# A graph layer's edge sort: joining the pieces of destination and weight on GpSimd instead of VectorE

## What is computed

```
hi, hj = h[src], h[dst]                       # 50000 rows each
x   = concat(hi, hj, edge_weight)
msg = layer_norm(silu(x @ mW1 + mb1))
msg = silu(msg @ mW2 + mb2)
agg = segment_sum(msg, src)                   # 3125 rows
y   = silu(concat(h, agg) @ uW1 + ub1) @ uW2 + ub2
```

## Time and profile before

| what | value |
|---|---|
| three executions | 1671.7, 1673.52, 1680.5 us |
| median | 1673.52 us |
| span of the profiled execution, first to last instruction | 1439.5 us |
| the profiled execution's own time | not listed apart from the three |
| median less span | 234.0 us |
| mean granted TensorE clock | 0.950 |

### The profile page before, as it was taken

How to read it: one execution, slowest core, us unless ns; L and a number is a source line. 1 busy time by engine, 2 the same in 40 slices (tenths; PEclk the granted TensorE clock), 3 DMA queues, 4 the chain that set the end, 5 groups by cost and what they waited for, 6 DMA issues and landing times.

```text
span 1439.5 us, 32698 instructions
## 1 busy us (share of the span) xinstructions
PE 1279.5 (89%) x8927; PEld 1149.6 (80%) x8928; DVE 1182.8 (82%) x3550; ACT 932.1 (65%) x1856; POOL 878.1 (61%) x885
## 2 busy tenths in 40 slices
PE   2678899996999999999999999999998847999990
PEld 1366778786999999999999999999886635988890
DVE  6999778726999999999999999999954688666662
ACT  0877444414778887888878888888753544666660
POOL 2188774035887778787777787878710014767761
PEclk7599999997999999999999999999999978999995
DMA  3911100022333333333333333336860162444447
GB/s 118 197 34 43 31 13 23 1 68 64 111 104 98 104 106 101 101 99 112 99 101 102 107 103 101 100 108 93 86 193 0 43 253 72 75 73 73 73 60 280
DMA packets 71387, 133.94 MB, mean 93 GB/s; under 512 B 23126, under 2 KB 43868, under 8 KB 70695
## 3 DMA queue, kind: packets, MB, share of 16 engines
q0 software_dynamic: 36560, 77.33, 24.1%
q1 hardware_dynamic: 33986, 52.62, 12.0%
q10 hardware_dynamic: 780, 3.24, 0.6%
HBM read 107.71 MB, written 25.29 MB: 92 GB/s over the span
## 4 chain that ended last, share of the span: by engine, by line
PE 71%; DVE 17%; DMA 4%; issue 3%; ACT 2%; POOL 1%; DVEq 0%; ACTq 0%; POOLq 0%; SPq 0%
PE ps L1071 12%; PE ps L832 9%; PE ps L1045 7%; PE ps L1049 7%; PE ps L1044 7%; PE ps L1061 7%; DVE place_val_t L1579 3%; DVE lane_hot_e_t L1574 2%; PE ps L1170 2%; PE ps L1201 2%; PE ps L1199 2%; PE ps L1200 2%; PE ps L1172 2%; PE ps L1171 2%; PE ps L1102 2%
## 5 line engine op out<-in xcount | busy, mean ns | idle before, releaser
L752 POOL DMA_INDIRECT msg_t<-dst_table,stage_idx x448 | 444.2, 991 | 128.7 <-issue 126.5
L1044 PE MATMUL ps<-w_hi_t,msg1T_hi_t 128*128 128x256 f32 x896 | 252.4, 303 | 0.0
L1338 ACT ACTIVATE msg1n_t<-msg_t,nw_b,nw_y 128x256 f32<-128x256 f32 x448 | 242.4, 590 | 0.0
L1350 ACT ACTIVATE msg_t<-msg_t 128x512 f32<-128x512 f32 x224 | 141.6, 632 | 149.4 <-DVE msg_t L1743 148.8
L1045 PE MATMUL ps<-w_lo_t,msg1T_hi_t 128*128 128x256 f32 x896 | 234.2, 283 | 0.0
L1071 PE MATMUL ps<-msg_t,hot_t 128*125 128x256 f32 x896 | 230.4, 379 | 0.2 <-issue 0.2
L1049 PE MATMUL ps<-w_hi_t,msg1T_lo_t 128*128 128x256 f32 x896 | 179.8, 282 | 0.0
L1045 PEld LDWEIGHTS ps<-w_lo_t,msg1T_hi_t 128*128 128x128 f32 x896 | 171.9, 192 | 0.0
L1044 PEld LDWEIGHTS ps<-w_hi_t,msg1T_hi_t 128*128 128x128 f32 x896 | 170.3, 190 | 0.0
L1738 DVE BATCH_NORM_STATS2 est<-msg_t 128x6 f32<-128x256 f32 x448 | 166.2, 413 | 1.2 <-ACT msg_t L1350 1.2
L1071 PEld LDWEIGHTS ps<-msg_t,hot_t 128*125 128x125 f32 x896 | 152.0, 187 | 14.2 <-issue 0.4
(11 more groups left out here) (374 smaller groups left out, 3081.1 us busy)
## 6 DMA issues: line engine op xcount, KB each, us to landing
near_rows<-row_list SPq DMA_DIRECT2D x44, 320.0 KB
w_sb_t<-in_L_ffn_W_dram SPq DMA_DIRECT2D x16, 512.0 KB, 8.5
msg_t<-dst_table,stage_idx POOLq DMA_INDIRECT x448, 2.8
res_t<-in_x_dram SPq DMA_DIRECT2D x1, 3125.0 KB
total<-zero_chunks_t SPq DMA_DIRECT2D x1, 3125.0 KB, 26.8
dst_table<-dst_stage SPq DMA_DIRECT2D x25, 125.0 KB
xm_table<-xm_t POOLq DMA_DIRECT2D x5, 625.0 KB, 7.5
sum_a_t<-total SPq DMA_DIRECT2D x5, 625.0 KB, 10.6
```

The source lines that it names most:

```text
L752: pool.indirect_dma_start(out=msg1[:, k, j, :], out_offset=None, in_=dst_table, in_offset=bass.IndirectOffsetOnAxis(stage_idx[:, G * k + j ...
L1044: pe.matmul(o[j], part(msg1T_hi, j, c), w2_hi[:, c, :], start=(c == 0), stop=False)
L1338: m = A(msg1n[:, (kl + 1) % 2, j, :], msg1[:, kk, j, :], ACT.Identity, bias=nw_b[:, kk, j:j + 1], scale=nw_y[:, kk, j:j + 1])
L1350: A(v, v, ACT.Silu).then_inc(msg1_sb, 1)
```

## The change

The three additions of `land(g)` move from VectorE to GpSimd, with a semaphore `landed` of their own. GpSimd's program becomes: for each group g, `land(g)`, then the three scatters numbered 3g-3 to 3g-1 (`BESIDE` is 3; none ahead of group 1); behind the loop the remaining scatters, 45 to 111. `part_w` gets two buffers at another place. ScalarE's copies of group g wait for `landed` of g-2. SP's row loads and VectorE's source table wait for all sixteen landings. The halves of the chunk numbers are summed in PSUM: two matmuls of one column for each run, 14 a group instead of seven of two columns, so VectorE has one addition left (`chunk_places`) and `run_to` goes. Two semaphores of the expert routing (`gap_ok`, `exp_ok`) become one, `softmax_ok`, with two values.

```diff
-        part_w = sort_use("part_w_t", [128, PLACES], F32)
+        part_w = at("part_w_t", [128, 2, PLACES], F32, "work", 15872)
...
@@ sync
             sp.wait_ge(chunk_ok, GROUPS)
-            sp.wait_ge(chunk_ps, GROUPS)
+            sp.wait_ge(landed, GROUPS)
...
@@ gpsimd
             pool.wait_ge(zeros_out, 16)
+
+            def land(g):
+                in_chunks = lambda t: t.rearrange("p (j c) -> p j c", c=CHUNK)
+                pool.wait_ge(sort_ok, g + 1)
+                st.did(pool.tensor_tensor(part_w[:, g % 2], pieces[:, g % 2, 3], pieces[:, g % 2, 4], ALU.add))
+                st.did(pool.tensor_tensor(sort_sb[:, g, :, :, 0], in_chunks(pieces[:, g % 2, 0]), in_chunks(pieces[:, g % 2, 1]),
+                                          ALU.add))
+                st.join()
+                pool.tensor_tensor(sort_sb[:, g, :, :, 2], in_chunks(part_w[:, g % 2]), in_chunks(pieces[:, g % 2, 5]), ALU.add)\
+                    .then_inc(landed, 1)
+
+            def scatter(g, j):
+                pool.wait_ge(landed, g + 1)
+                pool.wait_ge(chunk_ok, g + 1)
+                pool.indirect_dma_start(
+                    out=sorted_edges, out_offset=bass.IndirectOffsetOnAxis(chunk_to[:, g, j:j + 1], 0),
+                    in_=sort_sb[:, g, j].rearrange("p c f -> p (c f)"), in_offset=None).then_inc(scattered, 16)
+
+            BESIDE = 3
             for g in range(GROUPS):
-                pool.wait_ge(sort_ok, g + 1)
-                pool.wait_ge(chunk_ok, g + 1)
-                for j in range(RUNS):
-                    pool.indirect_dma_start(
...
+                land(g)
+                for q in range(BESIDE * g - BESIDE, BESIDE * g):
+                    if q >= 0:
+                        scatter(q // RUNS, q % RUNS)
+            for q in range(BESIDE * GROUPS - BESIDE, GROUPS * RUNS):
+                scatter(q // RUNS, q % RUNS)
@@ tensor
                 for j in range(RUNS):
-                    m = pe.matmul(bank(4 + g % 2, 2, first=2 * j), reached[0:NB + 1, g % 2, j * 128:j * 128 + 128],
-                                  group_h[0:NB + 1, g, :], start=True, stop=True)
+                    for h in range(2):
+                        m = pe.matmul(bank(4 + g % 2, 1, first=j), reached[0:NB + 1, g % 2, j * 128:j * 128 + 128],
+                                      group_h[0:NB + 1, g, h:h + 1], start=(h == 0), stop=(h == 1))
@@ scalar
                 act.wait_ge(sort_ps, g + 1)
-                after(act, chunk_ok, g - 1)
+                after(act, landed, g - 1)
@@ vector
-            def land(g):
...
+            def chunk_places(g):
                 dve.wait_ge(chunk_ps, g + 1)
-                ends = bank(4 + g % 2, 2 * RUNS).rearrange("p (j h) -> p j h", h=2)
-                st.did(dve.tensor_tensor(run_to[:], ends[:, :, 0], run_row[:], ALU.add))
-                st.join()
-                dve.tensor_tensor(chunk_to[:, g], ends[:, :, 1], run_to[:], ALU.add).then_inc(chunk_ok, 1)
+                dve.tensor_tensor(chunk_to[:, g], bank(4 + g % 2, RUNS), run_row[:], ALU.add).then_inc(chunk_ok, 1)
...
                 if g:
-                    land(g - 1)
-            land(GROUPS - 1)
+                    chunk_places(g - 1)
+            chunk_places(GROUPS - 1)
             dve.wait_ge(zeros_out, 16)
             dve.wait_ge(total_zero, 16)
+            dve.wait_ge(landed, GROUPS)
```

More of the change, by code:

```diff
@@ L329, in gps_layer @@
         run_row = s("run_row", [128, RUNS])
-        run_to = s("run_to", [128, RUNS])
         token = s("token", [128, TOPK * NB])
@@ L400, in gps_layer @@
             "reached_ok", "sort_in", "sort_ps", "sort_ok", "chunk_ps", "chunk_ok"))
-        scattered, table_ps = sem("scattered"), sem("table_ps")
+        scattered, landed, table_ps = sem("scattered"), sem("landed"), sem("table_ps")
         table_sb, side_out, xnT_lo_ok, w_hi_ok, w_lo_ok = (sem(n) for n in (
@@ L432, in gps_layer @@
             "var2_ok", "sd2_ok", "rstd2_ok", "xm_ok", "x2T_ps", "x2T_sb", "logit_ps"))
-        gap_ok, exp_ok, hotk_ok, route_ps, tile_ok = (sem(n) for n in (
-            "gap_ok", "exp_ok", "hotk_ok", "route_ps", "tile_ok"))
+        softmax_ok, hotk_ok, route_ps, tile_ok = (sem(n) for n in ("softmax_ok", "hotk_ok", "route_ps", "tile_ok"))
+        GAP_OK, EXP_OK = 1, 2
         logit_ok = sem("logit_ok")
@@ L1405, in _ @@
                 copy_xm(t, t // 4 + 1)
-            act.wait_ge(gap_ok, 1)
-            A(wtmp[0:NP], wtmp[0:NP], ACT.Exp).then_inc(exp_ok, 1)
+            act.wait_ge(softmax_ok, GAP_OK)
+            A(wtmp[0:NP], wtmp[0:NP], ACT.Exp).then_inc(softmax_ok, 1)
             act.wait_ge(w2_in, 16 * NE)
@@ L1553, in _ @@
             step(dve.tensor_tensor(edge(place_h), by_col(place_i), by_col(place_j), ALU.add))
-            def land(g):
[L1556 to L1559, removed]
-                st.did(dve.tensor_tensor(sort_sb[:, g, :, :, 2], part_w[:].rearrange("p (j c) -> p j c", c=CHUNK),
-                                         piece(5), ALU.add))
+            def chunk_places(g):
                 dve.wait_ge(chunk_ps, g + 1)
-                ends = bank(4 + g % 2, 2 * RUNS).rearrange("p (j h) -> p j h", h=2)
-                st.did(dve.tensor_tensor(run_to[:], ends[:, :, 0], run_row[:], ALU.add))
-                st.join()
-                dve.tensor_tensor(chunk_to[:, g], ends[:, :, 1], run_to[:], ALU.add).then_inc(chunk_ok, 1)
+                dve.tensor_tensor(chunk_to[:, g], bank(4 + g % 2, RUNS), run_row[:], ALU.add).then_inc(chunk_ok, 1)
             st.join()
@@ L1856, in _ @@
             st.join()
-            dve.tensor_tensor(wtmp[R], top_v[R, :, 1], top_v[R, :, 0], ALU.subtract).then_inc(gap_ok, 1)
+            dve.tensor_tensor(wtmp[R], top_v[R, :, 1], top_v[R, :, 0], ALU.subtract).then_inc(softmax_ok, 1)
             for k in range(TOPK):
@@ L1890, in _ @@
             st.did(dve.tensor_copy(slot_t[R], slot_q[R, 1]))
-            dve.wait_ge(exp_ok, 1)
+            dve.wait_ge(softmax_ok, EXP_OK)
             step(dve.tensor_scalar(wgt[R, 0, :], wtmp[R], 1.0, None, ALU.add))
```

2 lines of the change are left out of this document (removed).

## The result

The changed kernel takes 1680.94 us (median of 15 runs, 1673.45 to 1685.97), the kernel before, run beside it on the same chip, 1672.11 us (15 runs, 1665.47 to 1681.75). The ratio is 1.0051 [1.0031, 1.007]: the change costs about 9 us. The forecast was 1676.0 in a range of 1667 to 1682.

A forecast was written before the change was run, and what follows sets the result against it. The prediction took VectorE to bound the sort; its -6.5 us goes uncollected because GpSimd would end last, so +3.0 - 0.5 = +2.5 us on 1673.52 gave 1676.0 us, range 1667.0 to 1682.0.

The forecast's parts named there:

- Removed 0.61 a group: Sort, VectorE: moving the additions saves 0.61 us a group, 9.2 us over fifteen groups, the most the change can give.
- The port cost of three additions: Sort, VectorE: GpSimd's reads for 45 additions, priced by columns, cost VectorE 2.7 us, leaving it a net -6.5 us.
- The third rival: Sort: shared-port rule to the letter, VectorE loses each whole addition, 13.5 - 9.2 = +4.3 us, 1677.8; chance 0.07.
- matmuls at nothing: Sort, TensorE: seven more one-column matmuls add at most 0.2 us a group, hidden by its wait for place_val.
- So POOL becomes what ends the sort: 166.7: Sort's end: GpSimd's last landing at 166.7 us, against VectorE's src_lo start at 163.68 today: +3.0 us.
- the first rival: Sort: GpSimd keeps up in phase, last landing at 157.2, VectorE's gain of up to 6.5 us collected, 1667.0 to 1670.5; chance 0.22.
- The tail. ... The cover is 21 us; nothing to pay.: After the sort: last scatter at 255.8, table landed at 261.4, ScalarE reads it at 282.57, so the delay costs nothing.
- All later stages shift one for one: Stages after the sort: they keep their length and move by as much as the sort's end moves.
- The signs: Wrong if GpSimd's last landing comes before 158, its additions take over 0.6 us, or stages after the sort change length.
- 234.0 us "around the span": Whole kernel: the profiled span of 1439.5 us plus 234.0 us around it gives the median, 1673.52, untouched by the change.

The follow-up runs named there:

- pe_only: Kernel before, with only TensorE summing the halves of the chunk numbers and the three additions kept on VectorE: 1675.09 us, ratio 1.0026.
- base: The kernel before, unchanged, profiled once more: 1672.74 us, ratio 1.0012; the profiled execution has a span of 1675.0 us.
- land_only: Changed kernel with the chunk numbers as before and two buffers for run_to, so only the additions move to GpSimd: 1679.28 us, ratio 1.0051.
- beside0: Changed kernel with BESIDE = 0, all 112 scatters behind the sixteenth landing: 1730.77 us, ratio 1.0376.
- The pair with the bound: At most two scatters in flight, kernel before from group 8, changed kernel from its 46th scatter: 1604.52 us (0.9581) and 1612.43 us (0.9642).
- hold: Kernel before, with GpSimd waiting for the whole source table ahead of the scatters of group 8: 1657.06 us, ratio 0.9916.

## Why the prediction was right and wrong

**Right: VectorE's terms.** Removed 0.61 a group was 0.62. The port cost of three additions, priced by columns at 0.18 a group, was 0.23 (3.00 - 2.77). The end of place_val came 4.8 us earlier (152.9 against 157.7), where 6.5 was the sum over fifteen groups. The third rival, the rule to the letter, is refuted: the three additions last 0.25 + 0.56 + 0.42 = 1.23 on GpSimd and cost VectorE 0.23, not their whole length. (The Trainium skill, "SBUF — State Buffer", "Who interferes with whom", calls the shared port pair an exclusive lock. These rows agree that both sides wait: two of the three additions take 0.56 and 0.42 beside VectorE's products, all three of the last landing, with VectorE idle, 0.25. But VectorE does not lose the whole of what the profile records as the addition's length. The Trainium skill says "for the whole instruction" there of VectorE's two-port modes; of an instruction with both inputs in SBUF it says only that it contends.)

**Right as far as shown: matmuls at nothing.** pe_only has no longer period, and the landings alone cost what the change costs; pe_only's ratio of 1.0026 leaves room for a few us.

**Wrong: "So POOL becomes what ends the sort: 166.7".** The last landing ended at 157.6. A landing cost 1.26 and not 1.63: 16 x 0.37 = 5.9 us. I had taken the odds of meeting a VectorE instruction as if the two ran independently; they fell in phase, the first rival's condition, with its 157.2. And the count of scatters up to the last landing was 42, not 45, since `land(15)` stands ahead of the scatters 42 to 44: 3 x 1.62 = 4.9 us. Together that more than covers the 9.1 us of difference. So the sort went as rival 1 had it, though its 157.2 was met partly by luck: it too counts 45 scatters, and it takes 1.04 for a landing that cost 1.26; put right, the sum is 67.67 + 42 x 1.62 + 16 x 1.26 = 155.9. By that rival the time would have been faster; it was not, because of the next step.

**Wrong, and deciding: "The tail. ... The cover is 21 us; nothing to pay."** The landing of the table was the only thing that I let the last scatter delay. The runs show another: as long as scatters leave every 1.26 to 1.29 us, TensorE's counts reach ScalarE late, and the stage beside them stands. In base that stage ends 25 us behind the last scatter (231.3 to 256.2), so this end has no cover at all. The seventy scatters behind the last landing (67 in the prediction, by the same slip in the count), 1.29 us each, end at 247.7 (I had 255.8), which is 16.4 us after base's 231.3, and keys and values start 11.9 us later. The gain of the sort, 4 to 5 us, is lost in it: a tile that is ready earlier waits longer. What shows it are the starts of keys and values in seven profiles (11 us apart, as said above), land_only (same cost) and beside0 (last scatter 67 us later, time 60 us later). The pair with the bound shows that the crawl costs at least 4% of the time; it does not show that the change's loss goes with it, since 0.6% of it stays.

**"All later stages shift one for one"** held for keys and values (92 us in both), not for the source table (87 and 110 us).

**The signs.** Of the three that were to show the prediction wrong, two came: the last landing before 158 (157.6), and a stage after the sort that changed length. The third did not: no addition of the steady pattern took over 0.6 us (0.56).

**The ground.** The prediction was built on an execution in which the crawl doesn't show, though its scatters were nearly as dense (1.34 us apart on the mean of the tail), and I added 234.0 us "around the span" without asking what they were. In base only 1.8 us are around it, and the spans differ by 235.5 us, of which 82.0 are there when the edge loop starts (417.9 against 335.9) and 154.7 are added in it. A gap of 14% between span and time meant that the profile wasn't one of the timed executions, and that some stage took longer in those. It could be seen before. What makes an execution crawl or not was not found; that the old trace is the only complete one is a difference on record.

## What to carry to other kernels

Count what a change adds to the queue that ends last, even where its result is wanted late: the row of indirect DMAs disturbed whoever ran beside it. Where an engine idles on a "remote" release in a program of one core, look for a dense row of DMAs with completion counts, and try to space them out or to bound those in flight; here a few lines of waits on two semaphores brought 4% in the executions measured, many times what the change was after. Look first whether the trace is complete: here it was not wherever the crawl was. And a profile whose span is far from the median of the runs is to be taken again before anything is summed on it.

## What was not expected of the hardware

- In the traced executions a count of TensorE went up as much as 58 us after its matmul while scatters were issued every 1.26 us, each raising a count by 16 on completion (`then_inc(scattered, 16)`); ScalarE's counts for VectorE and VectorE's for TensorE took about 0.1 us at the same time (168.89 to 169.03, 169.45 to 169.51). That the sixteen increments of each scatter are what TensorE's stand behind is compatible with all runs (density, hold, bound), but no run shows where a count waits, or that it would wait without the recording. The Trainium skill, "DMA: Bandwidth & Descriptors", section "Why a DMA increments its semaphore by 16 and not by 1", says that all 16 DMA engines post a +1 for a DMA issued by GpSimd; the complete old trace agrees, with 1792 changes for 112 scatters.
- While the stage crawls, the clock falls to its lower level (the windows of base, 160 to 240 us: TensorE busy 14.03 of 80 us, granted clock 0.55 on the mean; from 168 to 240 us it is busy 9.89 of 72 us at 0.50, the lower level); the crawl's matmuls take 0.41 us where the same ones took 0.28.

```profile
160.00:240.00 80.00, 14.03 (x71) 11.91 (x68) 5.94 (x13) 3.09 (x9) 54.22 (x57) 0.55 0.05 8
```

- The edge loop, 224 units with two gathers each, shows the same kind of wait, here VectorE's for a count of TensorE: `msg_t` L1743 sat idle 3.6 us in the old profile and 140.5 in base, nearly all of it "remote" (92 waits, 2.2 us the longest), and a unit takes (1283.9 - 417.9) / 223 = 3.88 us instead of (1047.2 - 335.9) / 223 = 3.19. That is 155 us. The gathers weren't bounded in any run; whether that would give it back is open. The page's group in base:

```profile
L1743 DVE TENSOR_TENSOR msg_t<-ps,msg_t 128x512 f32<-128x512 f32 x224 | 152.9, 683 | 140.5 <-remote 132.6
```

- An addition of 128x28 takes GpSimd 0.25 us with VectorE idle, and between 0.25 and 0.56 beside VectorE's products.
